# Decoder layer on one core: the context's loads are issued by the ScalarE queue at the end of its round

## The chip, the cores and the metric

The kernel runs on one core of one Trainium2 chip. The metric is device time in microseconds (us). Three runs of the kernel before took 1537.62 to 1549.59 us, with a median of 1540.39 us.

The engines are PE (TensorE, matmuls; PEld is its weight load), DVE (VectorE), ACT (ScalarE), POOL (GpSimd) and SP (SyncE, which here only issues transfers). SPq, ACTq and POOLq are the same engines when they issue a DMA. All DMAs of the core run on the same 16 DMA engines.

## The reference

The function is one decoder layer on 32 independent sequences, in float32: `x` is (32, 100, 256) and the context `ctx_1024` is (32, 361, 256).

```python
x = layernorm(x + attn(x, ...))        # 16 heads of 16: causal window, plus 4 latent heads over pooled pairs, gated
x = layernorm(x + xattn(x, ctx, ctx))  # q, k, v projections, layernorm of q and k per head, softmax over 361 keys
x = layernorm(x + ffn(x, ...))         # 8 experts of 1024, top-1 routing, 200 rows each, scaled by pmax / pmax
```

For cross attention each sequence needs its context twice: the keys are projected, normalised per head and split into a high and a low f16 half, and the values are projected. Each query row is shifted by its maximum score before the exponential.

## The kernel before, in words

Work is pipelined over sequences in **rounds** numbered n = -2 to 33. A round does one stage for each of several sequences (`OFFSET`, line 57): stage A (self attention) for sequence n+2, stage B (the output of self attention and the cross queries) and K (the cross keys) for n+1, X (the maxima of the cross scores) and V (the values) for n, Y (the exponentials and the weighted sum) for n-1, and T (second norm and routing) for n-2. The middle rounds are a hardware loop of two rounds per pass. After the rounds, the eight experts run.

Each engine has its own instruction order, written out by hand in a function `body(it)`; engines meet at semaphores. An engine that waits holds everything behind it in its own order. That holds for SP too: its transfers are issued in the order of its body (lines 615 to 632):

1. `bounce_self`, `stack_self`: the split q and k of self attention go out to DRAM and come back in another layout (`self_stack`), 6 transfers. Used by PE at line 853.
2. `bounce_keys`: the split keys `Khl` go to DRAM (`key_halves`), once DVE has made the low half (`k_lo`).
3. `load_c(n+2)`: the context, 361 KB, into `cT[p]`. The same buffer is read by PE's last value matmuls of this round (`V56(it, [2])`, "V6"), so it waits for `filled["V6"]`.
4. `load_x(n+3)`: the transposed x, 100 KB, into `xT[p]`. It waits for `filled["A2"]` of the previous round. PE reads it in the first instructions of the next round (A1, lines 828 to 835).
5. `bounce_queries`: the split queries `Qhl` go to DRAM (`query_halves`), once POOL has made the low half (line 725).
6. `load_n`, then `stack_keys` (3 transfers into `stacked`) and `stack_queries` (3 transfers into `Qst`). PE waits for both at the first cross maximum of the next round (X0, lines 988 to 992).

PE's order at the end of a round is Y1 (line 1022), V6 (lines 825 and 826, "MI<-weights,cT"), A6 (905, 907), Y2 (1030), A7 (914). The next round begins with A1 and A2 ("MI<-xT,weights" and "MI<-weights,xT"), two score steps Y0 and Y1 around T2 (1009, 935), then X0 and X1 (line 991), and the first key projection K1 (lines 825 and 826, "MI<-cT,WkC"), which is the first reader of the context loaded a round earlier.

ACT's order at the end of a round is the copy out of V6 (line 1241), then the copy out of A6 into `OsT` (line 1163). Its next work is the first exponential of the next round (line 1207). ACT issues two small transfers in a round (lines 1224 and 1233).

Of the kernel before, what the change touches and what calls it, by code (L numbers as in the profile page):

```python
# [33 lines left out]
B, S, D = 32, 100, 256  # L34
M = 361
# [91 lines left out]
def held(eng, value):  # L127

    return value if isinstance(value, int) else eng.to_reg(value)
# [30 lines left out]
def decoder_kernel(nc, io):  # L160
    ctx = ExitStack()
    with ctx:
        def sb(name, shape, dt=F32):
            return ctx.enter_context(nc.sbuf_tensor(name, shape, dt))

        def sem(name):
            return ctx.enter_context(nc.semaphore(name))
# [145 lines left out]
        cT = [sb(f"cT{p}", [128, 2, M]) for p in range(2)]  # L313
# [86 lines left out]
        started = sem("started")  # L400
# [5 lines left out]
        loaded_c = [sem(f"loaded_c{p}") for p in range(2)]  # L406
        filled = {s: sem(f"filled_{s}") for s in MISC}
# [77 lines left out]
        def bank(step, it):  # L485
            return (count(MISC, step, it) - 1) % 2
# [36 lines left out]
        def _(sp):  # L523
# [1 line left out]
                sp.dma_start(tile[:], io[name]).then_inc(loaded_const, 16)  # L525
            sp.dma_start(biases[:], io["biases"].partition_broadcast(S)).then_inc(loaded_const, 16)

            def load_c(b):

                p, n = b.parity, b.index()  # L530

                after = held(sp, b.done(back=2))
                sp.wait_ge(started, 1)
                sp.wait_ge(filled["V6"], after)
                sp.dma_start(cT[p][:], io["cT"][:, :, bass.ds(n * M, M)]).then_inc(loaded_c[p], 16)  # L535

            def load_x(b):

                p, n = b.parity, b.index()
                after = held(sp, b.done(back=2))  # L540
                sp.wait_ge(started, 1)
                sp.wait_ge(filled["A2"], after)
                sp.dma_start(xT[p][:], io["xT"][:, :, bass.ds(n * S, S)]).then_inc(loaded_x[p], 16)

            def load_n(b):

                p, n = b.parity, b.index()
                after = held(sp, b.done(per=5, back=2))
                sp.wait_ge(started, 1)
                sp.wait_ge(b_pool, after)  # L550
                sp.dma_start(xn[p][:], io["x"][bass.ds(n * S, S), :]).then_inc(loaded_n[p], 16)
# [5 lines left out]
            def bounce_self(it):  # L557

                a = it.of("A")
                made, read = held(sp, a.done()), held(sp, a.done(per=80, back=1))  # L560
                sp.wait_ge(started, 1)
                sp.wait_ge(a_lo, made)
                sp.wait_ge(a_stack, read)
                sp.dma_start(self_halves.rearrange("h p n -> p h n"), QKhl[:]).then_inc(a_out, 16)

            def stack_self(it):

                a = it.of("A")
                out, free = held(sp, a.done(per=16)), held(sp, in_order(SCORES, "As2", it.before()) if it.n > FIRST else 0)
                sp.wait_ge(started, 1)  # L570
                sp.wait_ge(a_out, out)
                sp.wait_ge(st_full, free)
                rows = QKst.rearrange("p (t a) n -> p t a n", a=4)
                sp.dma_start(rows[0:32], groups(self_halves, HIGH, 3)).then_inc(a_stack, 16)
                for row in (1, 2):
                    for part_of, which in ((slice(0, 2 * S), Q_ROWS[row]), (slice(2 * S, 3 * S), K_ROWS[row])):
                        for_rows = rows[32 * row:32 * row + 32, :, :, part_of]
                        sp.dma_start(for_rows, groups(self_halves, which, 3)[:, :, :, part_of]).then_inc(a_stack, 16)
# [20 lines left out]
            def bounce_keys(it):  # L599
                bounce(it.of("K"), Khl, key_halves, k_lo, 2, k_out, k_stack)  # L600

            def stack_keys(it):
                b = it.of("K")
                stack(it, b, Kst[b.parity], Khl, key_halves, K_ROWS, k_out, k_stack)

            def bounce_queries(it):
                bounce(it.of("B"), Qhl, query_halves, b_ql, 1, b_out, b_stack)

            def stack_queries(it):
                b = it.of("B")  # L610
                stack(it, b, Qst[b.parity], Qhl, query_halves, Q_ROWS, b_out, b_stack)
# [3 lines left out]
            def body(it):  # L615
                if it.has("A"):
                    bounce_self(it)
                    stack_self(it)
                if it.has("K"):
                    bounce_keys(it)  # L620
                if it.n + 2 < B:
                    load_c(Seq(it.n + 2, it.j))
                if it.n + 3 < B:
                    load_x(Seq(it.n + 3, it.j))
                if it.has("B"):
                    bounce_queries(it)
                if it.n + 2 < B:
                    load_n(Seq(it.n + 2, it.j))
                if it.has("K"):
                    stack_keys(it)  # L630
                if it.has("B"):
                    stack_queries(it)
# [516 lines left out]
        def _(act):  # L1149
# [5 lines left out]
            def leave(ins, step, it):  # L1155
                ins.then_inc(emptied[bank(step, it)], 1)

            def copy_out(step, it, out, source, free=None):

                act.wait_ge(filled[step], it.of(step[0]).done())  # L1160
                if free:
                    act.wait_ge(*free)
                leave(act.activation(out, source(MI[bank(step, it)]), ACT.Copy), step, it)
# [35 lines left out]
            def cross_exp(it, u):  # L1199
                b, first = it.of("Y"), pair_of(f"Y{u}", it)  # L1200
                act.wait_ge(st_full, in_order(SCORES, f"Y{u}", it))
                if u == 0 and b.n == 0:
                    act.wait_ge(zeroed, 16)
                if u == 0:
                    act.wait_ge(filled["Y1"], b.done(back=1))
                n, width = (KN[0], 400) if u % 2 == 0 else (KN[2], 200)
                act.activation(cross_part(Px, u), ST[0:n, first:first + 2, 0:width], ACT.Exp).then_inc(st_exp, 1)  # L1207
# [37 lines left out]
            def gate_exp(it):  # L1245
                b = it.of("B")
                act.wait_ge(b_z, b.done(per=4, k=1))
                act.activation(gate_e[:], gate_z[:], ACT.Exp, scale=-1.0).then_inc(b_e, 1)
# [32 lines left out]
            def router_exp(it):  # L1281
# [3 lines left out]
                act.wait_ge(t_exp, b.done(back=1))  # L1285
                act.activation(exps8[:], logits[:], ACT.Exp, bias=negtop[:], accum_out=extra[:, bass.ds(b.index(), 1), 0:1].rearrange("p a d -> p (a d)")).then_inc(t_exp, 1)

            halves = lambda ps: ps[:, 0:2 * S].rearrange("p (t q) -> p t q", t=2)

            def body(it):  # L1290
                a, k, b, x, y, t, v = (it.has(stage) for stage in "AKBXYTV")
                if y: cross_exp(it, 0)
                if t: copy_out("T2", it, OxT[:], halves)
                if y: cross_exp(it, 1)
                if a: self_hi(it)
                if k: K12(it, 0)
                if y: cross_exp(it, 2)
                if b: copy_out("B1", it, latT[:], lambda ps: ps[0:64, 0:S])
                if y: cross_exp(it, 3)
                if t: rstd(it.of("T"), rs2, ln2, mv2, t_ln, t_rs)  # L1300
                if y: cross_exp(it, 4)
                if k: K12(it, 1)
                if b: gate_exp(it)
                if k: K34(it, 0)
                if y: cross_exp(it, 5)
                if t: copy_out("T4", it, x2T[:], halves)
                if b: copy_out("B3", it, mixT[:], halves)
                if k: high_k(it, 0); K34(it, 1)
                if y: cross_exp(it, 6)
                if a: A4(it)  # L1310
                if t: router_exp(it)
                if y: cross_exp(it, 7)
                if b: rstd(it.of("B"), rs1, ln1, mv1, b_ln, b_rs)
                if v: values(it, [0, 1])
                if b: copy_out("B5", it, x1T[:], halves)
                if k: high_k(it, 1)
                if a: self_exp(it, 0)
                if b: B6(it)
                if x: X1(it)
                if a: self_exp(it, 1)  # L1320
                if b: B7(it)
                if y: copy_out("Y1", it, OxU[:], lambda ps: ps[:, 0:4 * S], (filled["Y2"], it.of("Y").done(back=1)))
                if a: self_exp(it, 2)
                if b: high_q(it)
                if v: values(it, [2])
                if a: copy_out("A6", it, OsT[:], lambda ps: ps[:, 0:5 * S], (filled["A7"], it.of("A").done(back=1)))

            iterations(act, body)


# [445 lines left out]
```

## Time and profile before

| | |
|---|---|
| median of three runs | 1540.39 us |
| the profiled execution's own time | 1558.85 us |
| its span | 1557.0 us |
| PE busy | 1211.0 us (78%) |
| DVE / ACT / POOL busy | 842.6 / 673.5 / 335.7 us |
| mean granted TensorE clock | 0.903 |
| bytes moved by DMA | 134.99 MB, mean 87 GB/s |

The profiled execution took 1558.85 us and its span is 1557.0 us, so 1.85 us lie outside the span. It is 18.5 us above the median of the three runs. Busy time is an average over stages: PE is busy 78% of the span, but it also sits idle at fixed places of each round, and what counts is which wait ends last there. The granted clock has two levels, full (2.4 GHz) and half (1.2 GHz), shown as 1.00 and 0.50.

### The profile page before, as it was taken

Reading aid. Unit: us, or ns where it says so; the run is one execution under the profiler, and the core shown is the slowest. Engines: PE = TensorE matmul, PEld = TensorE weight load, DVE = VectorE, ACT = ScalarE, POOL = GpSimd, SP = SyncE. Lnnn points to the kernel's source line nnn. Section 1 sums busy time; section 2 is a strip of 40 time slices with the busy share of each in tenths; the row PEclk is TensorE's granted clock in tenths of the full one; section 3 lists DMA queues with packets and bytes.
Section 4 is the critical chain, followed back from the end, with each engine's and each line's share of the span. In section 5 each row is a group of like instructions: output and inputs, shape, how many; then the busy total and the mean of one; then the engine's idle time right before and its main releaser. Section 6 shows DMA issues by size and latency. Waiting matters only on the chain.

```text
span 1557.0 us, 33961 instructions
## 1 busy us (share of the span) xinstructions
PE 1211.0 (78%) x11098; PEld 881.9 (57%) x11098; DVE 842.6 (54%) x2482; ACT 673.5 (43%) x1611; POOL 335.7 (22%) x485
## 2 busy tenths in 40 slices
PE   3577777888778888888887888788878887675885
PEld 2355555555555555666555566565555565454774
DVE  4234456566665656565556665666566655433432
ACT  0123445444454445444545454555455545432110
POOL 2111112122222222222222222222212222100111
PEclk9667989899999989889999999999999989866998
DMA  4233332233333333333333333334333333106542
GB/s 152 50 78 70 83 85 62 64 86 86 75 84 84 84 84 84 84 84 82 85 78 86 78 77 81 87 74 91 76 84 84 84 83 76 45 10 211 194 148 72
DMA packets 187012, 134.99 MB, mean 87 GB/s; under 512 B 95798, under 2 KB 182762, under 8 KB 186734
## 3 DMA queue, kind: packets, MB, share of 16 engines
q1 hardware_dynamic: 181778, 127.50, 34.3%
q0 software_dynamic: 3200, 6.61, 1.4%
q8 instruction: 29, 0.48, 0.1%
q10 hardware_dynamic: 1984, 0.23, 0.1%
q14 instruction: 21, 0.17, 0.0%
HBM read 91.06 MB, written 43.00 MB: 86 GB/s over the span
## 4 chain that ended last, share of the span: by engine, by line
PE 32%; issue 15%; DVE 14%; DMA 9%; POOL 5%; ACT 4%; SPq 3%; DVEq 1%; POOLq 0%; ACTq 0%
PE MI L825 7%; PE MI L826 6%; DMA xT<-in_xT 5%; PE MI L1022 4%; PE MX L1138 4%; DVE negmax_x L1445 3%; DVE negmax_s L1438 2%; DVE Khl L1520 2%; PE ST L825 2%; PE ST L826 1%; DMA self_stack<-self_halves 1%; ACT QKhl L1214 1%; PE MX L853 1%; PE MI L971 1%; SPq L535 1%
## 5 line engine op out<-in xcount | busy, mean ns | idle before, releaser
L1445 DVE TENSOR_REDUCE negmax_x<-MX 100x1 bf16<-100x361 f32 x512 | 261.6, 529 | 108.9 <-PE MX L991 107.9
L1207 ACT ACTIVATE wide<-ST 128x800 f32<-128x800 f32 (+1 forms) x256 | 169.9, 665 | 345.8 <-PE ST L1009 345.0
L991 PE MATMUL MX<-stacked,Qst 96*128 96x361 f16 x512 | 154.8, 331 | 119.0 <-DVE negmax_x L1445 67.1
L991 PEld LDWEIGHTS MX<-stacked,Qst 96*128 96x128 f16 x512 | 53.0, 106 | 201.0 <-DVE negmax_x L1445 133.1
L825 PE MATMUL MI<-xT,weights 128*128 128x100 f32 (+1 forms) x320 | 78.0, 333 | 49.2 <-DMA xT<-in_xT 48.3
L719 POOL TENSOR_TENSOR QKhl<-QK,QKhl 128x900 f16<-128x900 f32 x32 | 60.5, 1890 | 256.2 <-ACT QKhl L1214 256.2
L1009 PE MATMUL ST<-Qst,stacked 112*128 112x200 f16 x768 | 112.1, 257 | 0.3 <-ACT wide L1207 0.3
L1416 DVE TENSOR_SCALAR QK<-MI,small,parity_s 128x100 f32<-128x100 f32 x128 | 42.6, 374 | 103.4 <-PE MI L826 99.4
L734 POOL TENSOR_TENSOR x_all<-x,bpv 100x256 f32 (+1 forms) x32 | 23.2, 725 | 342.5 <-DVE x L1496 342.5
L825 PEld LDWEIGHTS MI<-xT,weights 128*128 128x128 f32 (+1 forms) x320 | 56.7, 224 | 69.7 <-DMA xT<-in_xT 40.0
L1009 PEld LDWEIGHTS ST<-Qst,stacked 112*128 112x128 f16 x768 | 70.7, 102 | 29.2 <-issue 10.1
L725 POOL TENSOR_TENSOR Qhl<-Qx,Qhl 128x400 f16<-128x400 f32 x32 | 30.2, 945 | 235.6 <-ACT Qhl L1279 235.6
L1022 PE MATMUL MI<-wide,Vx 128*32 128x100 f32 (+1 forms) x3072 | 78.3, 260 | 0.0
L1022 PEld LDWEIGHTS MI<-wide,Vx 128*32 128x32 f32 (+1 forms) x3072 | 70.9, 115 | 7.5 <-issue 7.4
L826 PE MATMUL MI<-xT,weights 128*128 128x100 f32 (+1 forms) x320 | 74.2, 322 | 0.0
L853 PE MATMUL MX<-mask_q,identb 100*128 100x400 bf16 (+1 forms) x128 | 46.3, 453 | 30.0 <-DMA self_stack<-self_halves 26.2
L1438 DVE TENSOR_REDUCE negmax_s<-MX 100x8 bf16<-100x800 f32 x64 | 63.0, 984 | 4.2 <-PE MX L859 4.2
L1197 ACT ACTIVATE Ps<-ST 100x800 f32<-100x800 f32 x64 | 53.4, 834 | 24.7 <-PE ST L891 24.7
L825 PE MATMUL MI<-weights,cT 128*128 128x256 f32 (+1 forms) x192 | 63.7, 414 | 0.5 <-issue 0.5
L1502 DVE TENSOR_TENSOR qn<-qc,rsq 128x200 f32<-128x200 f32 x32 | 11.8, 368 | 92.6 <-ACT rsq L1266 92.6
L971 PE MATMUL MI<-early,small 128*128 128x361 f32 x128 | 60.1, 555 | 1.1
L826 PEld LDWEIGHTS MI<-xT,weights 128*128 128x128 f32 (+1 forms) x320 | 59.4, 229 | 0.0
(259 smaller groups left out, 2889.7 us busy)
## 6 DMA issues: line engine op xcount, KB each, us to landing
stacked<-key_halves SPq DMA_DIRECT2D x96, 180.5 KB, 4.7
self_halves<-QKhl SPq DMA_DIRECT2D x32, 450.0 KB, 2.9
cT<-in_cT SPq DMA_DIRECT2D x32, 361.0 KB, 3.7
key_halves<-Khl SPq DMA_DIRECT2D x32, 361.0 KB, 2.8
self_stack<-self_halves SPq DMA_DIRECT2D x64, 150.0 KB, 3.9
Qst<-query_halves SPq DMA_DIRECT2D x96, 100.0 KB, 4.3
early<-in_w SPq DMA_DIRECT2D x8, 1024.0 KB
self_stack<-self_halves SPq DMA_DIRECT2D x32, 225.0 KB, 3.7
```

The lines of the kernel that those rows point to most:

```text
L719: pool.tensor_tensor(QKhl[:, LOW], QK[:].rearrange("p t n -> p (t n)"), QKhl[:, HIGH], ALU.subtract).then_inc(a_lo, 1)
L825: pe.matmul(out, lhs(0), rhs(0), start=True, stop=False)
L826: return pe.matmul(out, lhs(1), rhs(1), start=False, stop=True)
L853: pe.matmul(MX[:, i, 0:n], identb[0:S], mask_q[:, 0:n], start=True, stop=True)
L971: pe.matmul(ps[:, 0:M], average[:], sqk[:, t], start=True, stop=True).then_inc(filled[step], 1)
L991: pe.matmul(MX[:, n % 2, 0:M], Qst[p][0:96, n * S:n * S + 128], Kst[p][0:96, n // 2 * M:(n // 2 + 1) * M], start=True, stop=True).then_inc ...
L1009: mm = pe.matmul(ST[:, first + i, c:c + 2 * S], Kst[p][:, k:k + 128], Qst[p][:, 2 * pair * S:2 * (pair + 1) * S], start=True, stop=True)
L1022: mm = pe.matmul(ps[VW * j:VW * (j + 1), g * S:(g + 1) * S], Vx[p][0:n, kt, 4 * g + j], Px[0:n, c:c + S], start=(kt == 0), stop=(kt == 2))
L1138: mm = pe.matmul(MX[0:S, s, 0:D], hT[:, m, s * S:(s + 1) * S], W2[p][:, m], start=(m == 0), stop=(m == 7))
L1207: act.activation(cross_part(Px, u), ST[0:n, first:first + 2, 0:width], ACT.Exp).then_inc(st_exp, 1)
L1438: dve.tensor_reduce(out[:, 2 * g:2 * g + 2], MX[0:S, :, 0:400].rearrange("p i (u k) -> p i u k", k=S), X, ALU.max, negate=True).then_inc(m ...
L1445: dve.tensor_reduce(negmax_x[:, n:n + 1], MX[0:S, n % 2, 0:M], X, ALU.max, negate=True).then_inc(max_read, 1)
```

## The change

`load_c` leaves SP's body and is put at the end of ACT's body. Its semaphores and its condition are the same: ACT waits for `filled["V6"]` of the same round, which it has already waited for at its copy out of V6.

```diff
@@ SP @@
-            def load_c(b):
-                p, n = b.parity, b.index()
-                after = held(sp, b.done(back=2))
-                sp.wait_ge(started, 1)
-                sp.wait_ge(filled["V6"], after)
-                sp.dma_start(cT[p][:], io["cT"][:, :, bass.ds(n * M, M)]).then_inc(loaded_c[p], 16)
...
                 if it.has("K"):
                     bounce_keys(it)
-                if it.n + 2 < B:
-                    load_c(Seq(it.n + 2, it.j))
                 if it.n + 3 < B:
                     load_x(Seq(it.n + 3, it.j))
@@ ACT @@
+            def load_c(b):
+                p, n = b.parity, b.index()
+                after = held(act, b.done(back=2))
+                act.wait_ge(started, 1)
+                act.wait_ge(filled["V6"], after)
+                act.dma_start(cT[p][:], io["cT"][:, :, bass.ds(n * M, M)]).then_inc(loaded_c[p], 16)
...
                 if a: copy_out("A6", it, OsT[:], lambda ps: ps[:, 0:5 * S], (filled["A7"], it.of("A").done(back=1)))
+                if it.n + 2 < B:
+                    load_c(Seq(it.n + 2, it.j))
```

On SP, from the key bounce to the stacks, in the second round of the loop, the order before was this (`ISA` rows only hold a semaphore wait, `filled_V6` is the wait for V6):

```order
L586 DMA key_halves<-Khl 128x2x722 [waits k_stack0,k_lo,started]
L535 ISA [waits filled_V6,started]
L535 DMA cT<-in_cT 128x2x361
L543 ISA [waits filled_A2,started]
L543 DMA xT<-in_xT 128x2x100
L586 DMA query_halves<-Qhl 128x2x400 [waits b_stack0,b_ql,started]
```

And this is the same place of the changed kernel:

```order
L577 DMA key_halves<-Khl 128x2x722 [waits k_stack0,k_lo,started]
L534 ISA [waits filled_A2,started]
L534 DMA xT<-in_xT 128x2x100
L577 DMA query_halves<-Qhl 128x2x400 [waits b_stack0,b_ql,started]
```

The load of x now stands directly behind the key bounce, with no wait for V6 in between.

On ACT, at the seam between two rounds of the loop, the changed kernel has this (before, the two rows with line 1284 are not there, and the rest is the same):

```order
L1268 ACTIVATE Qhl<-Qx 128x400 [waits b_out,b_q]
L1230 ACTIVATE Vx<-MI 105x16x16 [waits filled_Y1,filled_V6]
L1152 ACTIVATE OsT<-MI 128x500 [waits filled_A7,filled_A6]
L1284 ISA [waits filled_V6,started]
L1284 DMA cT<-in_cT 128x2x361
L1190 REGISTER_ALU
L1196 ACTIVATE wide<-ST 128x2x400 [waits filled_Y1,st_full]
```

The context's load stands between the last copy of a round and the first exponential of the next.

## Rows read from the trace of the kernel before

**Rows 1.** Waits of all engines: who waited for whom, us in total, times, longest.

```profile
PE MI L825 <- DMA xT<-in_xT: 48.3, 29, 4.3
PE MX L991 <- DMA Qst<-query_halves: 45.9, 21, 7.0
```

**Rows 2.** Waits of SP's own queue, same columns.

```profile
SPq L534 <- PE MI L826: 130.8, 30, 5.0
```

**Rows 3.** Timeline of SP, 792 to 806: start, length, us, DMA, count.

```profile
792.79 0.37 SPq L586 DMA_DIRECT2D key_halves<-Khl  x1
797.77 0.62 SPq L535 DMA_DIRECT2D cT<-in_cT  x1
798.63 0.59 SPq L543 DMA_DIRECT2D xT<-in_xT  x1
799.33 0.54 SPq L586 DMA_DIRECT2D query_halves<-Qhl  x1
802.76 1.87 SPq L597 DMA_DIRECT2D Qst<-query_halves  x3
```

**Rows 4.** Timeline of PE, the same stretch; idle time before it in brackets.

```profile
796.95 0.59 PE L826 MATMUL MI<-weights,cT 128*105 128x256 f32 x2
799.28 1.10 PE L914 MATMUL MI<-pick,OsT 128*100 128x68 f32 x10
801.91 0.47 PE L825 MATMUL MI<-xT,weights 128*128 128x100 f32 x2 [1.53 <-DMA xT<-in_xT]
808.44 0.47 PE L991 MATMUL MX<-stacked,Qst 96*128 96x361 f16 x2 [1.90 <-DMA Qst<-query_halves]
808.78 0.85 PE L825 MATMUL MI<-cT,WkC 128*128 128x361 f32 x2
```

**Rows 5.** Timelines of ACT and POOL, the same stretch.

```profile
798.64 0.59 ACT L1163 ACTIVATE OsT<-MI 128x500 f32<-128x500 f32 x1 [0.49 <-PE MI L907]
806.32 0.84 ACT L1207 ACTIVATE wide<-ST 128x800 f32<-128x800 f32 x1 [7.08 <-PE ST L1009]
797.96 0.94 POOL L725 TENSOR_TENSOR Qhl<-Qx,Qhl 128x400 f16<-128x400 f32 x1 [7.14 <-ACT Qhl L1279]
```

**Rows 6.** Windows, same stretch: us, busy of five engines, granted clock, DMA share, GB/s.

```profile
800.00:801.00 1.00, 0.38 (x5) 0.24 (x3) 0.69 (x4) 0.00 (x0) 0.94 (x1) 1.00 0.99 329
805.00:807.00 2.00, 1.54 (x20) 1.23 (x18) 2.00 (x8) 0.68 (x1) 0.00 (x0) 1.00 1.26 177
```

**Rows 7.** DMA issue of the page: count, KB each, us to landing.

```profile
cT<-in_cT SPq DMA_DIRECT2D x32, 361.0 KB, 3.7
```

**Rows 8.** Round 30, which loads no context and no x: SP, PE, two windows.

```profile
1356.40 0.36 SPq L586 DMA_DIRECT2D query_halves<-Qhl  x1
1364.34 0.76 PE L991 MATMUL MX<-stacked,Qst 96*128 96x361 f16 x2 [6.86 <-DMA Qst<-query_halves]
1357.00:1359.00 2.00, 0.48 (x4) 0.25 (x4) 0.00 (x0) 1.00 (x3) 1.03 (x1) 1.00 0.63 166
1361.00:1363.00 2.00, 0.00 (x0) 0.00 (x0) 0.00 (x0) 0.00 (x0) 0.00 (x0) 0.53 1.24 198
```

**Rows 9.** Timeline of PE in a late round: V6's last matmuls and X0.

```profile
222.20 0.59 PE L826 MATMUL MI<-weights,cT 128*105 128x256 f32 x2
236.64 0.47 PE L991 MATMUL MX<-stacked,Qst 96*128 96x361 f16 x2
```

**Rows 10.** PE from X0 to line 930 at half clock and at full clock.

```profile
192.43 0.47 PE L991 MATMUL MX<-stacked,Qst 96*128 96x361 f16 x2 [2.04 <-DMA Qst<-query_halves]
198.06 0.67 PE L930 MATMUL MI<-weights,latT 64*100 64x256 f32 x2
768.20 0.47 PE L991 MATMUL MX<-stacked,Qst 96*128 96x361 f16 x2 [1.67 <-DMA Qst<-query_halves]
772.67 0.67 PE L930 MATMUL MI<-weights,latT 64*100 64x256 f32 x2
194.00:197.00 3.00, 2.67 (x11) 1.62 (x10) 1.51 (x3) 1.99 (x4) 1.71 (x3) 0.50 0.40 154
```

## The prediction, made before the change was run

> **What bounds the kernel now.** I read the waits first. PE waits 48.3 us in all, 29 times, for the load of x at line 825, and 45.9 us, 21 times, for the stacked queries at X0 [rows 1]. SP waits 130.8 us, 30 times, for V6 before the context's load: 4.4 us a round in which all that is behind it, the load of x first, cannot go [rows 2].
>
> Then one regular round, V6's end to X0. V6 ends at 797.54 (796.95 + 0.59). SP issues the context at 797.77, x at 798.63, the query bounce at 799.33; the last query stack is issued by 804.63 [rows 3]. PE finishes A7 at 800.38, sits idle 1.53 us for x, starts A1 at 801.91, and after that work sits idle 1.90 us again before X0 at 808.44 [rows 4]. So there are **two idle times in one stretch**, and the second has a releaser of its own, the landing of `Qst`. From V6 to X0 it is 10.9 us, and the second wait would be there whatever A1 did.
>
> What sets that landing are the 16 DMA engines: their share is 0.99 just after the context starts and still 1.26 at 805 to 807, just before X0 [rows 6]. A share of 1 or more means that transfers queue. In this stretch pass the context (361 KB), x (100), the query bounce (200), n (100), the keys (3 times 180.5) and the queries (3 times 100), and the last one is what PE waits for.
>
> **The change, part by part.**
>
> *x goes early.* SP would issue x behind the key bounce, whose issue ends at 793.16 [rows 3], so at about 793.4. A flight of 3.3 us (from 798.63 to A1 at 801.91 [rows 3, 4]) lands it at 796.7, before A7 ends at 800.38. Even twice that flight, for sharing the engines with the key bounce, lands in time. The wait of 48.3 us should go: A1 starts at about 800.4, 1.5 us earlier.
>
> *What is late next.* The work from A1 up to X0 takes 4.6 us (808.44 - 1.90 - 801.91 [rows 4]), so PE would stand before X0 at about 805.1. If `Qst` lands as before, it waits 1.90 + 1.53 = 3.4 us there: the gain of a regular round is given back whole. What counts is the landing of `Qst`.
>
> *The landing of Qst.* Removed in front of it on SP: two issues (0.62 + 0.59 us) and x's bytes. But the query bounce needs POOL's low half, which ends at 798.90 (797.96 + 0.94 [rows 5]), so it can go at 799.0 and gains 0.33 us, no more. Added beside it: the context. ACT issues it after the copy into `OsT` ends at 799.23 [rows 5]; register work and 0.6 us of issue put it 1.6 us later than SP's 797.77. Before, it had the engines nearly for itself ahead of the query bounce; now it lies in the midst of bounce and stacks.
> Round 30 loads no context, no x and no n, and needs 7.94 us from the query bounce to X0 (1356.40 to 1364.34 [rows 8]); the regular round needs 9.11 (799.33 to 808.44). For the new round I add to 7.94 the context at the rate of 329 GB/s [rows 6], 1.1 us, and n, 0.3 us: 9.35 us, so X0 at 808.35, 0.1 us sooner. Lower bound: context and n cost nothing, since round 30's engines are only 0.63 busy at 1357 to 1359 [rows 8]; X0 at 806.9, 1.5 us sooner. Upper bound: nothing is saved and the context comes on top of 9.11; X0 at 809.2, 0.8 us later. I take -0.1 us, nearest to the sum of pieces, times 25 steady rounds: **-3 us**.
> The Trainium skill (DMA: Bandwidth & Descriptors, "Issuing engines are not separate DMA queues") says that transfers issued from SP, ACT and POOL run on the same 16 engines and interleave, so that a second issuing queue saves only issue time. By that rule the change would bring 0.33 us a round at best; it speaks against the change, and share 1.26 fits it.
>
> *Late rounds.* Of 31 rounds, 10 do not wait at X0, because PE itself was later. The worst takes 13.85 us from V6's end to X0 (222.20 + 0.59 to 236.64 [rows 9]), against 10.9. An earlier A1 gives back up to 2.9 us there. Most of the ten lie near 11, so I count a little under three such rounds: **-8 us**.
>
> *The clock.* Today idle time before X0 comes in two pieces, 1.53 and 1.90 us, with 4.6 us of matmuls between. After the change it is one piece of 3.4 us, directly before the part of the round that PE bounds. In round 30 a long idle time took the granted clock to half before X0 (0.53 at 1361 to 1363 [rows 8]), and after X0 at 192.43 it stood at 0.50 as well. The price is in two rows: from X0 to line 930 it is 5.63 us at half clock (192.43 to 198.06) and 4.47 at full clock (768.20 to 772.67) [rows 10], so 1.16 us. Some of a slow stretch will fall into the idle time itself, where it costs nothing: I take 0.9 us, in 8 of 10 of 25 steady rounds: **+18 us**. Bounds: 0 (it never falls) and 29 (always, full price).
> The Trainium skill (TensorE: Matmul & The Clock Gate, "HAM oscillation — how this bites in real kernels") tells of a kernel in which every wait for a DMA was followed by matmuls at half rate. It is the case of this term taken to every round, which is the first slower rival below.
>
> *ACT.* One more issue (0.62 us by SP's row) in each of 32 rounds. ACT is idle 7.08 us there, until 806.32 [rows 5]. Were that cover gone, it would cost 20 us. Nothing. Its wait for V6 is already met by its own copy out of V6, so nothing queues behind it.
>
> *The context's reader.* K1 starts at 808.78 [rows 4]. Issued by 800.0 and with 3.7 us to landing [rows 7], or twice that, the context is there at 807.4. Nothing, with over 1 us left. PE's A1 needs no more than x: POOL's pair sums move up with it.
>
> **Sum:** -3 - 8 + 18 = +7 us. The profiled execution took 1558.85 us in all, so this would be 1566 for its like. It stands 18.5 us above the median; from the median of 1540.4 us I forecast **1547 us**.
>
> **The rivals.** A measurement of this kernel can tell about 1% (15.4 us) from no change.
>
> 1. *Forecast, 0.37: the wait moves to X0 and the clock takes a bit.* 1547, own range 1537 to 1556.
> 2. *The wait moves to X0 and the clock stays as it is, 0.10.* -3 - 8: 1529 to 1535. For it: regular rounds with 1.90 us idle before X0 kept full clock.
> 3. *Faster, 0.18: Qst lands sooner.* Two queues keep the engines fuller than one and the context slips into gaps as in round 30's 0.63. At 0.7 us a round, half of the bound, and the clock at half price: -17 - 8 + 9 = -16, so 1524; at the bound of 1.5 us, 1505. Against it: share over 1 just before X0.
> 4. *Slower, 0.20: half clock behind X0 in nearly every round.* Place: X0 to line 930; price 1.16 us times 25 = 29, less 8 and 3: +18, so 1558, and up to 1575 where the slow stretch reaches into the score steps. It decides from the point where more than about 8 of 10 rounds show it at full price.
> 5. *Slower, 0.15: the context delays the stacks.* It interleaves with keys and queries instead of going ahead of them: +0.5 us times 25 = 12, less 8, plus the clock's 18: +22, so 1563; at the bound of 0.8 us, 1570.
>
> That the change doesn't do what it says is excluded by the order of SP and ACT.
>
> **How the numbers follow.** Slower by over 1% (over 1555.8): most of rivals 4 and 5 and the top of the forecast, 0.20 x 0.85 + 0.15 x 0.9 + 0.05 = 0.36. Faster by over 1% (under 1525.0): a good half of rival 3 and a little of 2, 0.12 + 0.02 = 0.14. Within 1%: 0.50. The range leaves out the bottom third of rival 3 and the top of 4 and 5: **1521 to 1572 us**.
>
> **What would show it.** x: the wait of PE line 825 for `xT` falls from 48.3 us to under 5. Given back: the wait of line 991 for `Qst` grows from 45.9 us to about 80. Landing: from V6's end to X0 in regular rounds stays at 10.9 +- 0.4 us; 10.2 would be rival 3, 11.4 rival 5. Clock: 0.50 granted in the 3 us behind X0 in most rounds, and little of it in A1 and A2; full clock there is rival 2. Late rounds: none over 12 us. The forecast is wrong if the other parts of the round, from X0 to the next V6, change by more than the clock does: then A1's start was on a path through ACT, POOL and the self attention's stacks that I hold to be slack.

## The result and the profile after

The changed kernel takes **1584.3 us** (median of 4 runs, 1574.6 to 1586.1), the kernel before 1544.6 us beside it on the same chip. The ratio is 1.025 [1.018, 1.031]: slower by 2.5%. The forecast was 1547 us with a range of 1521 to 1572, so the prediction was wrong: too small a loss.

The page of the kernel after (span, clock by slices, the queue on which ACT issues, and the issue of the context with its median time to landing) says:

```profile
span 1581.9 us, 33963 instructions
PEclk8667889899999899999999989989988998866998
q10 hardware_dynamic: 10688, 12.07, 2.8%
cT<-in_cT ACTq DMA_DIRECT2D x32, 361.0 KB, 3.9
```

The mean granted clock of the run is 0.881; the profiled execution before had 0.903. As a half-clock time, 2 x (1 - clock) x span, that is 377 us against 302. ACT now issues the 32 loads of the context, and they land in 3.9 us, against 3.7 before [rows 7].

The waits of PE, after (us in total, times, longest):

```profile
PE MX L980 <- DMA Qst<-query_halves: 107.7, 32, 7.0
```

The wait for x is gone from the list, and the wait for the stacked queries has gone from 45.9 us to 107.7 [rows 1], in every round now. SP's wait for V6 [rows 2] is gone as well; SP sits out that time at the query bounce instead, for POOL's low half:

```profile
SPq L576 <- POOL Qhl L714: 162.5, 32, 7.5
```

One regular round after the change, the same one as in rows 3 to 5. V6 ends at 835.74. SP's own timeline (start, us of issue, line, transfer):

```profile
830.99 0.36 SPq L577 DMA_DIRECT2D key_halves<-Khl  x1
831.69 0.61 SPq L534 DMA_DIRECT2D xT<-in_xT  x1
837.25 0.36 SPq L577 DMA_DIRECT2D query_halves<-Qhl  x1
838.48 1.90 SPq L588 DMA_DIRECT2D stacked<-key_halves  x3
840.50 1.87 SPq L588 DMA_DIRECT2D Qst<-query_halves  x3
```

x is issued 0.34 us behind the end of the key bounce's issue, and the query bounce 1.51 us behind V6 (it was 1.79). The last query stack is issued 6.63 us behind V6, against 7.1 [rows 3].

ACT, same round (in brackets the idle time ahead and what ended it):

```profile
836.84 0.59 ACT L1152 ACTIVATE OsT<-MI 128x500 f32<-128x500 f32 x1 [0.49 <-PE MI L896]
837.03 0.65 ACTq L1284 DMA_DIRECT2D cT<-in_cT  x1
842.82 0.84 ACT L1196 ACTIVATE wide<-ST 128x800 f32<-128x800 f32 x1 [5.39 <-PE ST L998]
```

The context is issued 1.29 us behind V6, in 5.39 us of idle time of ACT.

PE, same round, A1 to line 919 (the line that was 930), and the same two rows of an earlier round with X0 at 729.09:

```profile
838.51 0.46 PE L814 MATMUL MI<-xT,weights 128*128 128x100 f32 x2
842.79 0.34 PE L998 MATMUL ST<-Qst,stacked 112*128 112x200 f16 x2
846.40 0.47 PE L980 MATMUL MX<-stacked,Qst 96*128 96x361 f16 x2 [3.27 <-DMA Qst<-query_halves]
846.70 1.42 PE L814 MATMUL MI<-cT,WkC 128*128 128x361 f32 x2
852.58 0.67 PE L919 MATMUL MI<-weights,latT 64*100 64x256 f32 x2
...
729.09 0.47 PE L980 MATMUL MX<-stacked,Qst 96*128 96x361 f16 x2 [3.00 <-DMA Qst<-query_halves]
733.72 0.67 PE L919 MATMUL MI<-weights,latT 64*100 64x256 f32 x2
```

A1 starts without a wait. All that it gained stands before X0: 3.27 us idle, where it was 1.53 and 1.90 in two pieces [rows 4]. Behind X0 the K1 pairs take 1.42 us, and from X0 to line 919 it is 6.18 us; in the round of 729.09 it is 4.63. The windows of both rounds (busy time of PE, PEld, DVE, ACT, POOL, then the granted clock, the DMA share and GB/s) tell why:

```profile
843.00:845.00 2.00, 0.13 (x2) 0.00 (x0) 0.67 (x4) 2.00 (x4) 0.00 (x0) 1.00 1.26 192
846.40:850.00 3.60, 3.60 (x11) 2.08 (x12) 0.98 (x2) 0.63 (x2) 2.13 (x3) 0.55 0.34 128
729.00:733.00 4.00, 3.43 (x17) 2.14 (x18) 2.47 (x5) 1.86 (x4) 2.58 (x3) 1.00 0.31 115
```

Full clock while PE idles, nearly half (1.2 GHz) as soon as it works again; behind X0 at 729.09 the clock stayed full. That case is the exception now: in the 23 middle rounds (below) it is 2. All context matmuls together (ns: shortest, median, longest), kernel after:

```profile
L814 PE MATMUL MI<-cT,WkC x128: 464/808/938, 69.1 to 1359.1; 128*128 128x361 f32 x128
```

and kernel before:

```profile
L825 PE MATMUL MI<-cT,WkC x128: 464/467/808, 68.0 to 1334.2; 128*128 128x361 f32 x128
```

The median matmul there went from full to half clock, 467 to 808 ns.

**The ledger.** I take the same 23 middle rounds in both traces and cut each at V6's end and at X0:

| us a round | before | after | times 23 |
|---|---|---|---|
| V6's end to X0 | 10.97 | 10.56 | -9.4 |
| X0 to the next V6's end | 29.19 | 30.73 | +35.4 |
| sum | 40.16 | 41.30 | +26 |

The profiled executions differ by 24.9 us (1558.85 to 1583.7): 26.1 in these 23 rounds, 3.4 more behind them and 4.7 less ahead of them. The medians differ by 39.7; what lies between is the execution of before that was profiled, which is 14 us over its median. The explanation below is of the 25 us. Of the other 15 I have no trace, only that executions of before differ with their clock too (1534.4 us at 0.919, 1554.8 at 0.898).

### The profile page after: what moved, and what is told of

Its sections match the earlier page's. It is cut to its first block, busy times and chain, and to the rows that moved or that the text cites. A ratio compares the mean times of both kernels' runs of the same rounds, so it can differ in the third digit from the quotient of the medians.

```text
span 1581.9 us, 33963 instructions
## 1 busy us (share of the span) xinstructions
PE 1235.9 (78%) x11098; PEld 884.3 (56%) x11098; DVE 842.7 (53%) x2482; ACT 676.4 (43%) x1611; POOL 336.5 (21%) x485
## 4 chain that ended last, share of the span: by engine, by line
PE 38%; issue 29%; DVE 16%; POOL 6%; DMA 5%; ACT 4%; SPq 2%; DVEq 1%; POOLq 0%; ACTq 0%
PE MI L814 6%; PE MI L815 5%; PE MI L1011 4%; PE MX L1127 4%; DVE negmax_x L1445 3%; DMA Qst<-query_halves 3%; PE MX L980 2%; DVE negmax_s L1438 2%; DVE Khl L1520 2%; SPq L588 2%; PE ST L998 2%; PE MI L960 2%; PE ST L814 2%; PE ST L815 1%; PE MX L842 1%
## 5 line engine op out<-in xcount | busy, mean ns | idle before, releaser
L980 PE MATMUL MX<-stacked,Qst 96*128 96x361 f16 x512 | 168.7, 362 | 174.6 <-DMA Qst<-query_halves 107.7
L980 PEld LDWEIGHTS MX<-stacked,Qst 96*128 96x128 f16 x512 | 56.2, 113 | 267.5 <-DVE negmax_x L1445 133.3
L998 PE MATMUL ST<-Qst,stacked 112*128 112x200 f16 x768 | 121.0, 273 | 0.3 <-ACT wide L1196 0.3
L998 PEld LDWEIGHTS ST<-Qst,stacked 112*128 112x128 f16 x768 | 76.5, 109 | 41.1 <-issue 23.1
L1158 ACT ACTIVATE early<-MI,bkC 128x361 f32<-128x361 f32 x64 | 35.8, 560 | 147.4 <-PE MI L815 147.3
L814 PE MATMUL MI<-cT,WkC 128*128 128x361 f32 x128 | 72.4, 659 | 0.0
L815 PE MATMUL MI<-cT,WkC 128*128 128x361 f32 x128 | 70.9, 647 | 0.0
L814 PE MATMUL MI<-xT,weights 128*128 128x100 f32 (+1 forms) x320 | 67.7, 295 | 0.9 <-DVE bpv L1401 0.9
L698 POOL TENSOR_TENSOR gate_r<-rem,biases 100x256 f32<-100x256 f32 x32 | 23.2, 726 | 192.0 <-DVE rem L1461 192.0
L815 PE MATMUL MI<-xT,weights 128*128 128x100 f32 (+1 forms) x320 | 63.6, 282 | 0.0
## 6 DMA issues: line engine op xcount, KB each, us to landing
stacked<-key_halves SPq DMA_DIRECT2D x96, 180.5 KB, 5.0
```

The lines of the kernel that those rows point to most:

```text
L814: pe.matmul(out, lhs(0), rhs(0), start=True, stop=False)
L815: return pe.matmul(out, lhs(1), rhs(1), start=False, stop=True)
L980: pe.matmul(MX[:, n % 2, 0:M], Qst[p][0:96, n * S:n * S + 128], Kst[p][0:96, n // 2 * M:(n // 2 + 1) * M], start=True, stop=True).then_inc ...
L998: mm = pe.matmul(ST[:, first + i, c:c + 2 * S], Kst[p][:, k:k + 128], Qst[p][:, 2 * pair * S:2 * (pair + 1) * S], start=True, stop=True)
```

## The experiments

The theory: PE's idle time, now in one piece before X0, drops the granted clock behind it, and that is the loss. The main rival: the context, among the stacks, costs time by its bytes. `...` and `@@` mark what is left out of an edit. Times are medians; the ratio is to the kernel before in the same job (1541 to 1548 us). "The two parts" are V6's end to X0 and X0 to V6, in the same 23 rounds.

**1. x first, the context stays on SP.** Kernel before, with this alone:

```diff
-                if it.n + 2 < B:
-                    load_c(Seq(it.n + 2, it.j))
                 if it.n + 3 < B:
                     load_x(Seq(it.n + 3, it.j))
+                if it.n + 2 < B:
+                    load_c(Seq(it.n + 2, it.j))
```

> The context's load stays on SP; only the order on SP is changed, x's load ahead of the context's. Theory (clock): x is early, the 3.3 us of idle time before X0 come in one piece, and half clock follows behind X0, as in the changed kernel: 1570 to 1590 us, from V6's end to X0 about 10.7 us, from X0 to V6 over 30 us. Rival (queue): the loss comes from the context on ACT's queue (its bytes interleaved with the stacks, its issue on ACT); with the context back on SP it is gone: 1525 to 1550 us.

Measured: 1557.7 us, 1.012 [1.006, 1.017]; parts 10.38 and 30.50; PE waits 98.5 us for the queries. So an early x, with no second queue, already moves the wait to X0 and brings the half clock behind it (in 20 of the 23 rounds; 30.50 against 29.19). The mechanism holds, but the time lies between what I expected of the theory and of the rival. The changed kernel is 26 us slower than this one. The two profiled executions differ by 26.7 us: 23 x (0.18 + 0.23) = 9 in the 23 rounds, 11 ahead of them and 6 behind them, so the second queue has a share of the loss, or the early and late rounds do, which no run here tells apart.

**2. x late.** Kernel after, with x held for V6:

```diff
@@ load_x @@
+                late = held(sp, b.done(back=3))
+                sp.wait_ge(started, 1)
+                sp.wait_ge(filled["V6"], late)
```

> The context's load is on ACT as in the changed kernel, but x's load on SP waits for V6 again. Theory (clock): the idle time is cut in two again (about 1.0 us before A1, 2.0 to 2.5 us before X0), little half clock behind X0: 1530 to 1555 us. Rival (queue): as slow as the changed kernel, 1575 to 1590 us.

Measured: 1582.4 us, 1.024 [1.018, 1.031]; parts 10.67 and 31.27. A miss, and it decides nothing: x landed in time all the same, PE waited for the queries 106.7 us in all, in one piece a round, and the idle time was never split. It shows only what had made x late before: the context's issue and bytes ahead of it, not V6.

**3. Filler.** Kernel after, with matmuls of no use before X0, into a PSUM tile that X0 then overwrites:

```diff
@@ cross_maximum, n == 0, ahead of X0 @@
+                for _ in range(16):
+                    pe.matmul(MX[:, 0, 0:400], identb[0:S], mask_q[:, 0:400], start=True, stop=True)
```

> The changed kernel, and PE runs 16 matmuls of 400 columns in f16-size operands (bf16) into the bank of X0 just before it waits for the stacks; their results are overwritten. They take about 2.7 us at full clock of the 3.3 us of idle time. Theory (clock): X0 starts at the same 10.5 us behind V6, no half clock behind it, from X0 to V6 28.1 to 29.3 us instead of 30.7: 1510 to 1545 us. Rival (queue, or the other engines' path): the same as the changed kernel, 1580 us, or slower by what the matmuls take.

Measured: **1515.3 us**, 0.982 [0.975, 0.988]; parts 10.52 and 29.16; clock 0.925. PE's timeline and a window behind X0 (columns as above):

```profile
817.13 2.87 PE L979 MATMUL MX<-mask_q,identb 100*128 100x400 bf16 x16
820.69 0.47 PE L982 MATMUL MX<-stacked,Qst 96*128 96x361 f16 x2 [0.69 <-DMA Qst<-query_halves]
821.00 0.77 PE L814 MATMUL MI<-cT,WkC 128*128 128x361 f32 x2
...
820.50:824.50 4.00, 3.33 (x17) 2.12 (x18) 2.47 (x5) 1.86 (x4) 2.19 (x3) 1.00 0.31 115
```

PE has 2.87 us more to do in each round, X0 starts as before (10.52 against 10.56), and the kernel is 69 us faster than the changed one. None of the 23 rounds has half clock behind X0. Of the 54 us between this profiled execution and that of the changed kernel, 37 lie in the 23 rounds, nearly all of it behind X0. The loads are untouched. This decides it: the clock is the cause, and the change with the idle time filled beats the kernel before. What the same filler would bring to the kernel before was not run.

**4. Half of it.** As above with `range(8)`.

> The changed kernel with 8 filler matmuls instead of 16, 1.35 us, so 1.9 us of idle time is left before X0, as much as the kernel before had there. Theory (clock, by the length of the idle time): little half clock behind X0, 1515 to 1545 us. Rival (any wait for a DMA there brings half clock): 1570 to 1585 us.

```profile
818.27 1.52 PE L979 MATMUL MX<-mask_q,identb 100*128 100x400 bf16 x8
821.74 0.47 PE L982 MATMUL MX<-stacked,Qst 96*128 96x361 f16 x2 [1.96 <-DMA Qst<-query_halves]
821.50:825.50 4.00, 3.28 (x17) 2.10 (x18) 2.47 (x5) 1.86 (x4) 2.33 (x3) 1.00 0.31 115
```

Measured: 1522.6 us, 0.988 [0.984, 0.991]; parts 10.56 and 29.21. The 1.96 us idle before X0 in this round, the size that it had before [rows 4], leave full clock behind it; so it is in 16 of the 23 rounds (1.4 to 2.0 us idle), and in the other 7 (1.7 to 2.3 us) half clock follows. Half of the filler brings nearly all.

**5. Filler without ACT's queue.** Kernel of experiment 1 with 16 fillers.

> Both orders of the load compared without the clock: x first, context on SP, and the 16 filler matmuls before X0. If the context on ACT's queue itself costs (it interleaves with the stacks instead of going ahead), this is faster than the filler on the changed kernel (1515 us) by 0.2 us a round, 1505 to 1512 us. Rival (ACT's queue costs more than bytes, 1 us a round): 1485 us. If it costs nothing: 1515 us.

Measured: 1506.6 us, 0.977 [0.972, 0.981]; parts 10.37 and 29.11. With the clock out of play, the context on ACT's queue costs about 9 us against SP's (1515.3), with intervals of the two ratios that overlap, so that much at most is likely; 0.15 us a round of it lies before X0.

**6. Small context.** Kernel after, with 8 of 361 columns of the context loaded from the third sequence on (what is computed from it is then not the reference's):

```diff
@@ load_c @@
+                keep = M if b.j is None and b.n < 2 else 8
-                act.dma_start(cT[p][:], io["cT"][:, :, bass.ds(n * M, M)]).then_inc(loaded_c[p], 16)
+                act.dma_start(cT[p][:, :, 0:keep], io["cT"][:, :, bass.ds(n * M, keep)]).then_inc(loaded_c[p], 16)
```

> The changed kernel, but from the third sequence on only the first 8 of 361 columns of the context are loaded, so the keys and values of these sequences come from an old context. The issue on ACT stays, 98% of the bytes go. Theory: the bytes hold up the landing of Qst by 0.6 to 1.1 us: X0 9.5 to 10.0 us behind V6, the idle time before it 2.1 to 2.6 us, fewer slow stretches behind X0: 1510 to 1560 us. Rival (the context is hidden in gaps): X0 stays at 10.5, 1580 us.

Measured: 1552.9 us, 1.007 [1.004, 1.011]; parts 10.09 and 30.53. Without nearly all of its bytes X0 comes 0.47 us sooner, under the 0.6 to 1.1 that I expected, and 2.5 to 2.9 us idle remain: the half clock stays in 20 of the 23 rounds. The bytes do count, 31 us by the medians and 0.67 us a middle round, but the kernel before moved them as well. The kernel without them is still no faster than the kernel before, so they alone do not explain the loss; what the move to ACT's queue costs is asked by experiment 5, not by this one.

**7. x behind the query bounce.** Kernel after; meant to part the idle time again:

```diff
                 if it.has("K"):
                     bounce_keys(it)
+                if it.has("B"):
+                    bounce_queries(it)
                 if it.n + 3 < B:
                     load_x(Seq(it.n + 3, it.j))
-                if it.has("B"):
-                    bounce_queries(it)
```

> The changed kernel with x's load issued behind the query bounce, so that x lands 2 us after A7 and PE's idle time is cut in two again: about 2.2 us before A1 and 1.0 to 1.5 us before X0. Theory (clock): X0 at the same 10.6 us behind V6, but from X0 to V6 28 to 29.5 us as in the kernel before, 1530 to 1555 us. Rival (the loss comes from the context on ACT's queue): 1575 to 1590 us.

Measured: 1600.3 us, 1.041 [1.035, 1.046]; parts 12.14 and 29.75. A clear miss, and a useful one:

```profile
776.97 0.75 PE L814 MATMUL MI<-xT,weights 128*128 128x100 f32 x2 [2.72 <-DMA xT<-in_xT]
784.60 0.47 PE L980 MATMUL MX<-stacked,Qst 96*128 96x361 f16 x2
778.00:784.00 6.00, 6.00 (x31) 4.95 (x31) 1.71 (x6) 0.00 (x0) 0.00 (x0) 0.53 0.65 101
```

x is now 2.72 us late, and the whole idle time stands before A1. The clock falls there: A1 to X0 runs at 0.53, PE busy throughout, and X0 is late by PE's own work. The half clock hit the work on the path from V6 to X0 instead of the work behind X0. The idle time did this at both places. The kernel before had it here too, in 9 of its 23 rounds (see below).

**8. Keys early.** Kernel after, with the key stacks issued before the query bounce:

```diff
                 if it.n + 3 < B:
                     load_x(Seq(it.n + 3, it.j))
+                if it.has("K"):
+                    stack_keys(it)
                 if it.has("B"):
                     bounce_queries(it)
                 if it.n + 2 < B:
                     load_n(Seq(it.n + 2, it.j))
-                if it.has("K"):
-                    stack_keys(it)
```

> The changed kernel with the three key stacks issued on SP right behind the key bounce and the load of x, instead of behind the query bounce. Theory: the landing of Qst, held up by the keys' 541 KB ahead of it on the 16 DMA engines, is what sets X0; without them X0 starts 7.5 to 8.5 us behind V6 instead of 10.6, the idle time shrinks under 1 us and the half clock goes with it: 36 to 37.5 us a round, 1430 to 1480 us in all. Rival (SP's sequencer or POOL's low half sets the landing, not the bytes): X0 at about 10 us behind V6, 1560 to 1580 us.

Measured: **1472.7 us**, 0.959 [0.952, 0.966]; parts 8.46 and 28.86; clock 0.930. SP's timeline, PE's X0, and the two windows before it:

```profile
778.42 1.90 SPq L588 DMA_DIRECT2D stacked<-key_halves  x3
781.85 0.37 SPq L577 DMA_DIRECT2D query_halves<-Qhl  x1
784.45 1.89 SPq L588 DMA_DIRECT2D Qst<-query_halves  x3
...
788.49 0.47 PE L980 MATMUL MX<-stacked,Qst 96*128 96x361 f16 x2 [0.76 <-DMA Qst<-query_halves]
784.00:786.00 2.00, 2.00 (x16) 1.55 (x15) 1.06 (x5) 0.00 (x0) 0.20 (x1) 1.00 0.75 250
786.00:788.00 2.00, 1.73 (x20) 1.41 (x20) 1.91 (x8) 0.59 (x1) 0.00 (x0) 1.00 0.65 147
```

The key stacks (3 times 180.5 KB) used to go out between the query bounce and the query stacks. Now they fill the time in which SP waits for POOL (the 162.5 us above). The DMA share before X0 falls from 1.26 to 0.65, X0 comes 2.1 us sooner, about 0.8 us idle remain, and the clock behind X0 stays full in all 23 rounds.

**9. Keys early, context on SP.** The same with the case's move taken back: the context on SP, behind the key stacks and ahead of the query bounce.

> The key stacks early as in the 1473 us kernel, but the context's load stays on SP, between the key stacks and the query bounce: order key bounce, x, key stacks, context, query bounce, n, query stacks. Theory (the bytes ahead of Qst count, not the issuing engine): as fast as with the context on ACT, or up to 10 us faster, because the context goes ahead of the query bounce while the engines are idle: 1460 to 1475 us. Rival (SP's issue time is the bound, ACT's queue is what makes the early stacks pay): 1490 to 1510 us.

Measured: 1529.8 us, 0.989 [0.983, 0.994]; parts 9.62 and 30.36. SP and PE:

```profile
781.51 0.61 SPq L535 DMA_DIRECT2D cT<-in_cT  x1
782.63 0.38 SPq L586 DMA_DIRECT2D query_halves<-Qhl  x1
786.53 1.89 SPq L597 DMA_DIRECT2D Qst<-query_halves  x3
790.50 0.48 PE L991 MATMUL MX<-stacked,Qst 96*128 96x361 f16 x2 [1.91 <-DMA Qst<-query_halves]
```

I had expected it near experiment 8, and it is 57 us slower. With the context ahead in its own queue, the query bounce lets the query stacks go 3.9 us behind itself, against 2.6 in experiment 8. So the move of this case does pay, 1.16 us a round before X0 and the clock on top, once the keys are out of the way.

This run shows one thing more. Its idle time before X0 is one piece of 1.9 to 2.4 us in 20 of the 23 rounds, no longer than in the kernel before, and yet 18 of the 23 rounds have half clock behind X0. One of them:

```profile
1111.55 0.48 PE L991 MATMUL MX<-stacked,Qst 96*128 96x361 f16 x2 [2.03 <-DMA Qst<-query_halves]
1112.70:1116.00 3.30, 2.97 (x12) 1.57 (x11) 1.53 (x4) 1.87 (x4) 2.31 (x3) 0.55 0.37 140
```

**10 to 12. On top of experiment 8.** (10) `load_n` up beside `load_x`; (11) that and 5 fillers; (12) as (10), with the third query stack issued by ACT, behind the context.

> The 1473 us kernel (context on ACT, key stacks early) with the load of n moved up beside x's. It takes 100 KB and an issue of 0.3 us out from between the query bounce and the query stacks. Theory (bytes ahead of Qst): X0 0.2 to 0.4 us earlier, 1462 to 1470 us. Rival (the query bounce's own landing sets it): no change, 1473 us.

> The 1470 us kernel (context on ACT, key stacks and n early) with 5 filler matmuls, 0.8 us, in the 0.9 us of idle time left before X0. Theory (clock, by the length of the idle time): under 1 us of idle time brings no half clock behind X0, so there is nothing to win: 1462 to 1478 us, the same. Rival (every idle time counts): 1440 to 1455 us.

> The 1470 us kernel with the third of the three query stacks issued by ACT, which is idle then, at the same time as SP's first. With the engines no longer full (share 0.65 to 0.75 in the 4 us before X0), SP's three issues of 0.62 us should be what sets the landing: X0 0.4 to 0.6 us earlier, 1452 to 1462 us. Rival (the engines still set it): no change, 1465 to 1475 us.

Measured: 1470.2 us (no ratio: its four runs lie 28 us apart, 1451.7 to 1479.7); 1471.2 us, 0.951 [0.945, 0.957]; 1457.0 us, 0.945 [0.939, 0.950]; parts 8.54 and 28.86, 8.59 and 28.76, 8.42 and 28.69. By the parts, the place of n is worth nothing (8.54 and 28.86 against 8.46 and 28.86), and the filler nothing once the wait is short. The third stack goes out in parallel with the other two:

```profile
778.79 1.21 SPq L588 DMA_DIRECT2D Qst<-query_halves  x2
778.81 0.62 ACTq L1295 DMA_DIRECT2D Qst<-query_halves  x1
```

That brought X0 0.12 us sooner, where I had expected 0.4 to 0.6; that the time still fell into the range that I gave is in part luck. Number 12 has the best time, 5.5% under the kernel before, but its lead over 11 is not settled: their intervals overlap.

## Why the prediction was wrong

**The step that failed is "The clock".** I took 0.9 us in 8 of 10 of 25 rounds, +18 us, with 29 as the upper bound. The 23 rounds show +35.4 behind X0. Three things were mis-sized:

- *How often.* 21 of 23 rounds have half clock behind X0, not 8 of 10.
- *The price.* The slow stretch hardly falls into the idle time, as I had assumed it would: the clock is full while PE idles (1.00 at 843 to 845) and falls between 0.9 us ahead of X0 and 0.6 us behind it. From X0 to line 919 a round pays up to 6.18 - 4.63 = 1.55 us, and over all of X0 to V6 one stretch costs about 1.3 (28.13 us without, 29.4 with) to 1.5 (30.9 with a second one late in the round).
- *How long.* In 4 of the 21 rounds the clock stays at half from X0 on for over 11 us, and X0 to V6 takes 32.7 us. I had bounded the term by a short stretch.

**Where the half clock fell before.** I read the two idle pieces of the kernel before as if both left full clock. They do in the round of rows 4, but in 9 of the 23 rounds half clock follows the first one, the wait for x, and A1 to X0 runs slow. One of them, with V6's end at 716.77:

```profile
721.42 0.47 PE L825 MATMUL MI<-xT,weights 128*128 128x100 f32 x2 [1.81 <-DMA xT<-in_xT]
727.61 0.47 PE L991 MATMUL MX<-stacked,Qst 96*128 96x361 f16 x2
722.80:726.20 3.40, 3.40 (x14) 2.43 (x14) 1.71 (x6) 0.00 (x0) 0.00 (x0) 0.51 1.17 192
```

That was nearly free: in 7 of the 9, X0 starts 10.6 to 11.1 us behind V6, as in the others, since the slow work only fills the wait for the stacks (no idle time ahead of X0 here, 10.84 us). No round of the 23 has half clock within 6 us behind X0. So the change moved the slow stretch, with the idle time, from work that had a wait behind it to work that has none. The length of the idle piece alone does not decide it: pieces of 1.5 to 2.4 us before X0 left full clock in every middle round before, and pieces of 1.9 to 2.4 us mostly did not in experiment 9. Which idle time brings half clock stays open.

Before, 16 of the 23 rounds already had one stretch, 22 to 25 us behind V6 (29.4 us where it was the only one, 27.8 to 28.1 without any). The change did not bring that one: after, 13 rounds have it behind the new one, and in the 4 long rounds the new one runs on nearly up to its place. So the new loss is about 17 x 1.4 = 24 for the short stretches and 4 x (32.7 - 29.4) = 13 for the long ones, 37 us; the difference measured is 35.4. With the filler of experiment 3 the late stretch is there still and the early one isn't: 29.16 us, the 29.19 of before.

The windows of such a long stretch, in the round with X0 at 929.54, kernel after:

```profile
929.50:933.00 3.50, 3.46 (x9) 2.05 (x10) 0.98 (x2) 0.25 (x1) 2.07 (x3) 0.50 0.35 132
933.00:937.00 4.00, 3.67 (x14) 1.99 (x11) 1.51 (x3) 1.74 (x4) 0.00 (x0) 0.50 0.63 116
937.00:941.00 4.00, 4.00 (x11) 2.21 (x11) 2.72 (x7) 1.78 (x4) 1.56 (x3) 0.50 0.41 57
944.00:948.00 4.00, 2.99 (x25) 1.71 (x24) 2.77 (x6) 3.52 (x8) 0.72 (x1) 1.00 0.00 0
```

PE is busy for 11.1 of 11.5 us, and its clock stands at half all that time. Why it came back so late here and after a few us elsewhere stays open; no run tells why. So does the cause of the late stretch that both kernels have.

I had read the clock of before at few places only. Had I cut all 23 rounds of it, X0 to V6 between 28 and 31 us would have shown what a stretch costs in a whole round.

My fourth rival was this mechanism, at 0.20, with 1558 and a bound of 1575; both were too low for the same reason, a price of 1.16 us and no long stretch. The Trainium skill (TensorE: Matmul & The Clock Gate, "HAM oscillation — how this bites in real kernels") tells of this pattern in a whole kernel; the trace agrees, with half clock behind 21 of 23 waits, though these waits, of 2.8 to 3.4 us, are shorter than most of those that it tells of.

**The other steps**, by the trace:

- *x goes early*: right. No wait is left, and A1 starts where A7 ends.
- *The gain is given back at X0*: right, 2.8 to 3.4 us a round against 3.4. My total of 80 us was low, since I counted only regular rounds: every one of 32 waits, 107.7 us.
- *The landing of Qst*: -0.33 us a round instead of -0.1 in the 17 of the 23 rounds that had waited at X0 (10.89 became 10.56), inside its bounds. The -9 us of the ledger hold this and about 2.6 us of two late rounds (11.76 and 11.80 became 10.35 and 10.57).
- *Late rounds*: I wrote that most of the ten lie near 11; that was a misreading, six of them took 11.76 us or more. The first four rounds, three of them late, gave -5.6 us (12.58, 10.67, 13.85 and 13.05 became 12.08, 10.96, 10.89 and 10.59); with the two above it is about -8. That this is the forecast number is luck, since the count behind it was wrong. One is over 12 still.
- *ACT*: right, nothing. *The context's reader*: right, no wait for `cT` on PE.
- *Rival 5* (the context delays the stacks): wrong in the kernel as changed, whose X0 comes sooner. Experiments 5 and 6 find its share, 0.15 us by the queue and 0.5 by the bytes; the early x, which alone takes V6 to X0 from 10.97 to 10.38 us (experiment 1), covers the first.
- *The condition that I named* (X0 to V6 changes by more than the clock does): with the clock held up by filler it is 29.16 us, against 29.19 before. A1's start was on no other path.

With the measured terms the sum is -9 + 35 = 26 for the middle rounds, and 25 between the two profiled executions, as the ledger has it.

## What to carry to other kernels

Before an early load is counted as a gain, ask where PE's idle time will stand afterwards: two waits of 1.5 and 1.9 us were cheaper than one of 3.3. The half clock behind the first fell on work that had a wait behind it; behind the long one it fell on the work that bounds the round, and in nearly every round. Price a clock term by whole rounds with and without a half-clock stretch, not by the few us behind the wait. And look at what the late transfer queues behind: the key stacks, moved into SP's own wait, brought more (112 us over the changed kernel) than the filler (69 us), and only then did the second queue pay.

## What the runs showed of the hardware

- Matmuls of no use made a kernel faster by 4.4% (1584.3 to 1515.3 us), 8 of them by nearly as much (1522.6).
- Idle time before X0 and half clock within 6 us behind X0, in the same 23 rounds: changed kernel, 2.8 to 3.4 us, 21 rounds; experiment 6, 2.5 to 2.9 us, 20; experiment 9, 1.9 to 3.1 us, 18; experiment 4, 1.4 to 2.3 us, 7; kernel before, 0 to 2.4 us, none; experiment 3, 0 to 0.7 us, none. From 1.9 to 2.4 us the runs differ, so these do not give a limit.
- The clock stayed at half for over 11 us with PE busy for 11.1 of 11.5.
- ACT began to issue the context at 837.03, while its copy (836.84 + 0.59) was still running; I had placed the issue behind it.
- Where a load stands in its queue seems to count although the 16 engines are shared: the same context ahead of the query bounce on SP put X0 1.16 us later than on ACT's queue (experiments 9 and 8). The query bounce itself was issued 1.42 us behind V6 in the one and 1.52 in the other, so it is not SP's issue time; no run shows it apart from where in the round the context starts. The Trainium skill (DMA: Bandwidth & Descriptors, "Issuing engines are not separate DMA queues") has it that a second issuing queue saves issue time only; the issue is 0.61 us, and these two runs differ by more than that.
